# Expert lists two to eight: scattered to a table in memory instead of found by one-hot products

## The chip, the cores and the metric

One core of a Trainium2 chip runs the whole program. The metric is the device time in microseconds (us), median of several runs.

## The reference

Two stages on x of 4 x 512 rows of 512 numbers (2,048 tokens). The first adds a gated product of the normalised, FP8-rounded rows with an FP8-rounded context. The second, which the change concerns, is a mixture of experts: a router picks two of eight experts for every token, an expert takes at most 640 tokens in order of arrival, and each token gets back the gated sum of its experts' outputs.

```python
C = math.ceil(CAPACITY_FACTOR * S * K / E)           # 640
probs = jax.nn.softmax(xr @ Wg, axis=-1)
gate_vals, expert_idx = jax.lax.top_k(probs, K)
flat_e = expert_idx.reshape(-1)
oh = jax.nn.one_hot(flat_e, E, dtype=jnp.int32)
pos = jnp.sum((jnp.cumsum(oh, axis=0) - 1) * oh, axis=1)
kept = pos < C
...
dispatched = xr[dispatch_mask.reshape(-1) % S].reshape(E, C, d)
h = jax.nn.relu(jnp.einsum('ecd,edf->ecf', dispatched, w1))
expert_out = jnp.einsum('ecf,efd->ecd', h, w2)
```

So every expert needs a list: for each of its 640 slots, which token stands there and with what gate.

## The kernel before

The engines run in parallel, each through its own program, and meet at semaphores. TensorE is PE, VectorE is DVE, ScalarE is ACT, GpSimd is POOL, and SyncE is SP.

**The front** (to about 179 us) computes attention, norms and router. The lists come at its end. `choose` marks the two experts of each token; `place` counts on PE, which leaves each token's position in each expert; `places` and `gates` on DVE turn that into `slots` (position plus one, or 0) and `marks` (token number plus one, and the gate as a high and a low half float). The first expert's list is found apart: DVE writes 16 one-hot tiles (L1357), PE multiplies them with the marks (L589 the tokens, L599 the gates), `first_rows` and `first_gates` on DVE read the result.

**An expert** is one pass of a loop on all engines; the eighth pass is written out behind it. Its first part is 16 tiles of hidden units, f = 0 to 15. PE does 12 matmuls a tile (L817), ACT writes the high half of the result (L1102) and splits w2 (L1105), DVE writes the low half (L1534), the low half of w2 (L1537), and looks for the largest weight of the next expert's w1 (L1312). Within these tiles lies the search for the next expert's list: DVE compares slot numbers 1 to 640 with the tile's slots (`onehot_tile`, L1417), PE multiplies the one-hot with the marks of 128 tokens (`find`, 5 matmuls, L578).

The second part multiplies with w2 (`second`, L750), four slot groups of 128, with a small piece for the slots above 512 (`first_rows` L729, `turn_rows` L738, L790) if the expert has so many. `turn_rows` stands in the middle of the second group and waits for `low_rest` on DVE (L1552). DVE's order at the start of this part is: wait for the five `acc` gathers, copy the gates, `read_list` (L1424 to L1431), `w_scales` (L1299 to L1303, which waits for POOL's all-reduce of the weight peak), two reduces over w2 (`peak_w2`, L1316), `combine(0)` (L1547), `low_rest(0)`.

**POOL** works in the order that it is written in. Before the loop it gathers the first expert's rows (L448, five indirect DMAs of 128 rows) and the rows that its results are added to (L454, five more). A pass of the loop is: all-reduce of the w1 peak (L438), gather of the next expert's rows (L448), scatters of the results (L461), all-reduce of the w2 peak, and the gather of the rows for the next addition (L454). SP loads the weights of the next expert; its first load of that kind waits until the fifth row gather has landed.

At the end of the front DVE splits w1 of the first expert in four pieces (`low_w1`, L1321, 128 x 2048 each), two before `first_gates` and two behind it; PE needs all four, and four transposed slot groups (`turn_slots`, L609, copied by ACT), before the first tile.

Of the kernel before, what the change touches and what calls it, by code (L numbers as in the profile page):

```python
# [19 lines left out]
F32 = mybir.dt.float32  # L20
# [70 lines left out]
def build(nc, x, ctx_in, g_xattn, g_ffn, wg, w1, w2, out, xsplit):  # L91
    with ExitStack() as stack:
# [16 lines left out]
        w2_t = w2.rearrange("e (f p) d -> e p f d", p=P)  # L109
        wg_t = wg.rearrange("(k p) e -> p k e", p=P)  # L110
# [84 lines left out]
        slots = sb("slots", [P, E, NT], F32)  # L195
        marks = sb("marks", [P, E, NT, 3], F16)
        slot_now = sb("slot_now", [P, NT], F32)
        marks_now = sb("marks_now", [P, NT, 3], F16)
        onehot = sb("onehot", [P, 2, C], F16)
# [83 lines left out]
        pool_passed dve_passed pe_passed picked onehot_ready found_done found_read idx_ready  # L283
# [17 lines left out]
        FIND_STEPS, SCALE_STEPS = 3, 3  # L301
# [71 lines left out]
        def _(pool):  # L373
# [3 lines left out]
            for t, v in ((ident32, 0.0), (ident16, 0.0), (before, 0.0), (ones16, 1.0), (ones32, 1.0), (lower_e, 0.0),  # L377
                         (warm, 1.0)):
                last = nc.gpsimd.memset(t[:], v)
            last.then_inc(q["const_base"], 1)  # L380
            pool.wait_ge(q["const_base"], 1)
            for t in (ident32, ident16):
# [8 lines left out]
            nc.gpsimd.iota(marks[:, :, :, 0], [[0, E], [P, NT]], base=1, channel_multiplier=1,  # L391
# [74 lines left out]
            gather_x(0, first=True)  # L466
            pool.wait_ge(q["rows_out"], 16 * B)
# [22 lines left out]
        def _(pe):  # L490
# [82 lines left out]
            def find(n, i):  # L573
                if i == 0:
                    pe.wait_ge(q["found_read"], n + 1)
                pe.wait_ge(q["onehot_ready"], n * NT + i + 1)
                for s in range(NS):
                    mm = pe.matmul(found_ps[:, s, :], onehot[:, i % 2, s * P:(s + 1) * P], marks_now[:, i, :],  # L578
                                   start=(i == 0 and s == 0), stop=(i == NT - 1), skip_group_check=True)
                mm.then_inc(q["found_done"], 1)  # L580

            def find_rows(i0, i1):

                for i in range(i0, i1):
# [3 lines left out]
                    for s in range(NS):  # L588
                        mm = pe.matmul(found_ps[:, s, 0:1], first_onehot(i)[:, s * P:(s + 1) * P], marks[:, 0, i, 0:1],  # L589
                                       start=(i == 0 and s == 0), stop=(i == NT - 1), skip_group_check=True)  # L590
                    mm.then_inc(q["found_done"], 1)

            def find_gates():
# [3 lines left out]
                for i in range(NT):  # L597
                    for s in range(NS):
                        mm = pe.matmul(found_ps[:, s, 1:3], first_onehot(i)[:, s * P:(s + 1) * P], marks[:, 0, i, 1:3],  # L599
# [209 lines left out]
            def expert(e, last):  # L809
# [3 lines left out]
                for f in range(NF):  # L813
# [6 lines left out]
                    if not last:  # L820
                        find(e + 1, f)
# [312 lines left out]
        def _(dve):  # L1134
# [233 lines left out]
            def places():  # L1368
# [4 lines left out]
                V.scalar_tensor_tensor(slots[:, :, :].rearrange("p e i -> p i e"), place_ps[:, 0:NT, :], 1.0,  # L1373
                                       chosen[:, :, :], ALU.add, ALU.mult)
# [6 lines left out]
            def gates():  # L1381
# [7 lines left out]
                high = marks[:, :, :, 1].rearrange("p e i -> p i e")  # L1389
                prep.step(V.tensor_copy(high, prob[:, :, :]))  # L1390
                V.tensor_tensor(marks[:, :, :, 2].rearrange("p e i -> p i e"), prob[:, :, :], high,
                                ALU.subtract).then_inc(q["first_list"], 1)
# [13 lines left out]
            def pick(n, steps):  # L1406

                V.tensor_copy(slot_now[:, :], slots[:, bass.ds(n, 1), :].rearrange("p o i -> p (o i)"))
                V.tensor_copy(marks_now[:, :, :].rearrange("p i c -> p (i c)"),
# [220 lines left out]
```

## Time and profile before

| | us |
|---|---|
| median of 3 runs | 901.55 (901.01 to 903.36) |
| the profiled execution | 899.0 |
| its span, first to last instruction | 897.2 |
| PE busy | 822.8 (92%) |
| DVE busy | 643.1 (72%) |
| ACT busy | 365.4 (41%) |
| POOL busy | 196.5 (22%) |

The span lies 1.8 us under the time of the same execution. Busy times are those of instructions; an engine can have nothing to do and cost nothing, so the shares alone don't say what bounds the program.

### The profile page before, as it was taken

How to read it: one execution, taken by the hardware profiler on the slowest of the kernel's cores; microseconds unless marked ns; L12 is line 12 of the kernel's file. 1: busy time of each engine (PE TensorE's matmuls, PEld its weight loads, DVE VectorE, ACT ScalarE, POOL GpSimd, SP SyncE). 2: the span in 40 equal slices, each digit the busy share in tenths (PEclk: the TensorE clock that was granted, in tenths of full speed). 3: DMA queues.
4: the chain of work that ended last, by engine and by line, in shares of the span. 5: the costliest groups of instructions: out<-in, count | busy, mean ns of one | idle time of the engine just before them, and what ended most of it. 6: DMA issues, size and time to landing. Idle time of an engine off the chain costs nothing.

```text
span 897.2 us, 13430 instructions
## 1 busy us (share of the span) xinstructions
PE 822.8 (92%) x4809; PEld 400.3 (45%) x4810; DVE 643.1 (72%) x1119; ACT 365.4 (41%) x587; POOL 196.5 (22%) x165
## 2 busy tenths in 40 slices
PE   0287989499999999999999999999999999999996
PEld 0134558344444444444444444444444444444443
DVE  5999868768596877788688578857885878585530
ACT  3798996334133441444043414331432144224410
POOL 2132331500232023203220232023202320232001
PEclk9999996599999999999999999999999999999999
DMA  8600734382456266328542763265328532702000
GB/s 302 260 0 1 259 116 171 93 290 95 125 163 211 101 145 234 123 94 175 219 147 98 129 223 123 105 145 211 120 97 169 206 123 94 175 24 70 1 26 22
DMA packets 77753, 123.05 MB, mean 137 GB/s; under 512 B 41870, under 2 KB 41886, under 8 KB 73632
## 3 DMA queue, kind: packets, MB, share of 16 engines
q1 hardware_dynamic: 68032, 93.33, 32.4%
q0 software_dynamic: 9696, 29.39, 11.4%
q8 instruction: 15, 0.25, 0.1%
q14 instruction: 10, 0.08, 0.0%
HBM read 96.49 MB, written 18.87 MB: 129 GB/s over the span
## 4 chain that ended last, share of the span: by engine, by line
PE 80%; DVE 10%; ACT 4%; DMA 2%; issue 2%; POOL 1%; SPq 0%; DVEq 0%; POOLq 0%; ACTq 0%
PE mm L750 37%; PE mm L817 36%; PE mm L790 2%; PE mm L729 2%; PE marks_ps L578 1%; ACT region L874 1%; DVE region L1183 1%; DVE region L1194 1%; DVE region L1225 1%; DVE region L1221 1%; DMA gains<-in_g_ffn 1%; POOL region L448 1%; DMA w_stage<-in_L_ffn_w 1%; PE mm L521 1%; PE mm L549 1%
## 5 line engine op out<-in xcount | busy, mean ns | idle before, releaser
L817 PE MATMUL mm<-region,w_split 128*128 128x512 f16 x1536 | 347.7, 380 | 1.7 <-ACT region L971 1.4
L750 PE MATMUL mm<-region 128*128 128x512 f16 x1536 | 335.8, 379 | 0.0
L750 PEld LDWEIGHTS mm<-region 128*128 128x128 f16 x1536 | 148.2, 98 | 179.7 <-issue 4.5
L817 PEld LDWEIGHTS mm<-region,w_split 128*128 128x128 f16 x1536 | 142.3, 98 | 159.8 <-issue 3.8
L1102 ACT ACTIVATE region<-mm 128x512 f16<-128x512 f32 x128 | 76.4, 597 | 323.3 <-PE mm L817 323.3
L1534 DVE SCALAR_TENSOR_TENSOR region<-mm,region 128x512 f16<-128x512 f32 x128 | 88.5, 691 | 88.1 <-ACT region L1102 88.1
L461 POOL DMA_INDIRECT out<-region,back_now x40 | 64.9, 1623 | 168.6 <-DVE region L1547 141.3
L1537 DVE SCALAR_TENSOR_TENSOR region<-w_stage,w_scale,region 128x512 f16<-128x512 f32 x128 | 96.5, 754 | 0.0
L1105 ACT ACTIVATE region<-w_stage,w_scale 128x512 f16<-128x512 f32 x128 | 91.2, 712 | 0.0
L438 POOL PARTITION_ALL_REDUCE peak_all<-peak x14 | 4.9, 349 | 352.9 <-DVE peak L1292 299.1
L1312 DVE TENSOR_REDUCE top<-w_stage 128x1 f32<-128x512 f32 x112 | 75.9, 678 | 2.9 <-DMA w_stage<-in_L_ffn_w 2.9
L1321 DVE SCALAR_TENSOR_TENSOR w_split<-w_stage,w_scale,w_split 128x2048 f16<-128x2048 f32 x32 | 73.8, 2348 | 1.7 <-DVE region L1563 1.7
L1547 DVE SCALAR_TENSOR_TENSOR region<-mm,gate_now,region 128x512 f32<-128x512 f32 x32 | 23.9, 748 | 59.0 <-PE mm L750 58.9
L1316 DVE TENSOR_REDUCE top<-w_stage 128x1 f32<-128x2048 f32 x28 | 62.6, 2275 | 0.0
L859 ACT ACTIVATE w_split<-w_stage,w_scale 128x2048 f16<-128x2048 f32 x32 | 61.6, 1991 | 0.0
L1552 DVE SCALAR_TENSOR_TENSOR region<-mm,region 128x512 f16<-128x512 f32 x32 | 22.1, 691 | 54.1 <-ACT region L1113 54.1
L1113 ACT ACTIVATE region<-mm 128x512 f16<-128x512 f32 x32 | 19.2, 599 | 100.6 <-PE mm L729 60.4
L448 POOL DMA_INDIRECT region<-x_split,row_next x40 | 43.8, 1095 | 48.7 <-issue 25.2
L454 POOL DMA_INDIRECT region<-out,row_next x40 | 39.6, 990 | 29.1 <-DMA out<-region,back_now 19.0
L1417 DVE TENSOR_SCALAR onehot<-slot_iota,slot_now 128x640 f16<-128x640 f16 x112 | 42.1, 381 | 0.9
L578 PEld LDWEIGHTS marks_ps<-marks_now,onehot 128*128 128x128 f16 x560 | 30.4, 96 | 27.2 <-DVE onehot L1417 1.1
L874 ACT ACTIVATE region<-region 128x128 f32<-128x128 f32 x128 | 38.8, 388 | 4.2 <-DVE region L1188 4.1
(188 smaller groups left out, 620.9 us busy)
## 6 DMA issues: line engine op xcount, KB each, us to landing
w_stage<-in_L_ffn_w SPq DMA_DIRECT2D x64, 1024.0 KB, 5.4
region<-in_x SPq DMA_DIRECT2D x4, 1024.0 KB, 13.4
x_split<-region SPq DMA_DIRECT2D x8, 512.0 KB, 3.8
out<-region SPq DMA_DIRECT2D x4, 1024.0 KB, 7.4
w_stage<-in_ctx SPq DMA_DIRECT2D x2, 1024.0 KB, 12.4
region<-in_ctx SPq DMA_DIRECT2D x2, 1024.0 KB, 15.5
region<-x_split,row_next POOLq DMA_INDIRECT x40, 4.5
region<-out,row_next POOLq DMA_INDIRECT x40, 3.8
```

Of the source, the lines that this page charges most:

```text
L448: pool.indirect_dma_start(x_slots[:, s, :], None, xsplit, bass.IndirectOffsetOnAxis(ap=row_next[:, s:s + 1], axis=0)).then_inc(x_got[s], 16)
L461: pool.indirect_dma_start(out_rows, bass.IndirectOffsetOnAxis(ap=back_now[:, s:s + 1], axis=0), acc[:, s, :], None, bounds_check=S - 1, oo ...
L750: mm = pe.matmul(mm2[s % 2][:, :], hidden[:, hh, f, s * P:(s + 1) * P], w2_split[:, wh, f, :], start=(f == 0 and hh + wh == 0), stop=(f == ...
L817: mm = pe.matmul(products(f), w1_split[:, wh, k, f * P:(f + 1) * P], xT[:, xh * KD + k, 0:WIDE], start=(k == 0 and wh + xh == 0), stop=(k ...
L859: nc.scalar.activation(w1_split[:, 0, k, :], w1_stage[:, k, :], ACT.Copy, scale=w_scale[:, 0:1]).then_inc(q["w1_hi"], 1)
L1102: nc.scalar.activation(hidden[:, 0, f, 0:WIDE], products(f), ACT.Relu).then_inc(q["hidden_hi"], 1)
L1105: nc.scalar.activation(w2_split[:, 0, f, :], w2_stage[:, f, :], ACT.Copy, scale=w_scale[:, 1:2]).then_inc(q["w2_hi"], 1)
L1312: return V.tensor_reduce(top1[:, i:i + 1], part, X, ALU.max, apply_absolute_value=True)
L1316: return V.tensor_reduce(top2[:, k:k + 1], w2_stage[:, WF * k:WF * (k + 1), :].rearrange("p f d -> p (f d)"), X, ALU.max, apply_absolute_v ...
L1321: V.scalar_tensor_tensor(w1_split[:, 1, k, :], w1_stage[:, k, :], w_scale[:, 0:1], w1_split[:, 0, k, :], ALU.mult, ALU.subtract).then_inc( ...
L1534: V.scalar_tensor_tensor(hidden[:, 1, f, 0:WIDE], products(f), 0.0, hidden[:, 0, f, 0:WIDE], ALU.max, ALU.subtract).then_inc(q["hidden_don ...
L1537: V.scalar_tensor_tensor(w2_split[:, 1, f, :], w2_stage[:, f, :], w_scale[:, 1:2], w2_split[:, 0, f, :], ALU.mult, ALU.subtract).then_inc( ...
```

## The change

The one-hot search for experts two to eight is gone, on PE and on DVE. In its place every token writes two notes of 8 bytes (token number plus one, gate) into a table `lists` in memory, one entry for each expert and slot. Where a note goes is its code, expert times 640 plus position; `places` computes the codes, `notes_of_rows` on DVE picks the larger and the smaller one of each token with its gate, and POOL sends 32 indirect DMAs of 128 notes before the loop. The table is filled with zeros at the start. In the loop POOL loads one expert's 640 entries with a plain DMA at the top of a pass, and `read_list` reads them from there; it now stands behind `w_scales`. The first expert's list is found as before.

```diff
+            for i in range(NT):
+                for w in range(2):
+                    pool.indirect_dma_start(
+                        lists, bass.IndirectOffsetOnAxis(ap=goals[:, w, i:i + 1], axis=0), notes[:, w, i, :], None,
+                        bounds_check=E * C - 1, oob_is_err=False).then_inc(q["lists_out"], 16)
             pool.wait_ge(q["rows_out"], 16 * B)
-            pool.wait_ge(q["first_list"], 1)
             gather_acc()
+            pool.wait_ge(q["lists_out"], 16 * 2 * NT)
             with nc.gpsimd.Fori(0, E - 1) as e:
+                pool.dma_start(entries[:, :, :], lists_t[e + 1]).then_inc(q["entries_in"], 16)
                 weight_peak(0, e + 1)
...
-                    if not last:
-                        find(e + 1, f)
...
-                V.scalar_tensor_tensor(slots[:, :, :].rearrange("p e i -> p i e"), place_ps[:, 0:NT, :], 1.0,
-                                       chosen[:, :, :], ALU.add, ALU.mult)
+                prep.step(V.scalar_tensor_tensor(codes[:, :, :], place_ps[:, 0:NT, :], 1.0,
+                                                 first_code[:, :].unsqueeze(1).broadcast_to([P, NT, E]), ALU.add, ALU.add))
+                prep.step(V.tensor_tensor(codes[:, :, :], codes[:, :, :], chosen[:, :, :], ALU.mult))
...
+            def notes_of_rows():
+
+                prep.step(V.tensor_reduce(code_of[:, 0, :], codes[:, :, :], X, ALU.max))
+                prep.step(V.tensor_reduce(code_of[:, 1, :], codes[:, :, :], X, ALU.add))
+                prep.step(V.tensor_tensor(code_of[:, 1, :], code_of[:, 1, :], code_of[:, 0, :], ALU.subtract))
+                for w in range(2):
+                    here = here_gates[:, w, :, :]
+                    prep.step(V.tensor_tensor(here, codes[:, :, :], over(code_of[:, w, :], E), ALU.is_equal))
+                    prep.step(V.tensor_tensor(here, here, prob[:, :, :], ALU.mult))
+                    V.tensor_reduce(notes[:, w, :, 1], here, X, ALU.add)
+                prep.step(V.tensor_scalar(unused[:, :, :], code_of[:, :, :], 0.0, 2 * SKIP, ALU.is_equal, ALU.mult))
+                V.scalar_tensor_tensor(goals[:, :, :], code_of[:, :, :], -1.0, unused[:, :, :], ALU.add,
+                                       ALU.add).then_inc(q["notes_ready"], 1)
...
             first_gates()
+            notes_of_rows()
             low_w1(0, 2)
...
                 for f in range(NF):
-                    if not last and f + 1 < NT:
-                        onehot_tile(n, f + 1, n * NT + f)
...
                 if not last:
+                    w_scales(n, 0, e * 2 * SCALE_STEPS)
                     read_list(n)
-                    w_scales(n, 0, e * 2 * SCALE_STEPS)
```

On POOL, the end of the front and the top of the loop read as follows before. The bracket is what an instruction waits for; the first L438 row, marked ISA, stands ahead of the all-reduce itself and carries its wait.

```order
L448 DMA region<-x_split,row_next 128x1024 x4
L454 DMA region<-out,row_next 128x512 [waits first_list,rows_out]
L454 DMA region<-out,row_next 128x512 x4
L470 UNCONDITIONAL_BRANCH
L470 ISA
L438 ISA [waits peak1_in]
L438 ISA peak_all<-peak 128x1
```

And now:

```order
L461 DMA region<-x_split,row_next 128x1024 x4
L484 DMA lists<-notes,goals 5120x2 [waits notes_ready,zeros_in]
L484 DMA lists<-notes,goals 5120x2 x31
L467 DMA region<-out,row_next 128x512 [waits rows_out]
L467 DMA region<-out,row_next 128x512 x4
L490 UNCONDITIONAL_BRANCH [waits lists_out]
L490 ISA
L491 DMA entries<-lists 128x5x2
L451 ISA [waits peak1_in]
L451 ISA peak_all<-peak 128x1
```

The 32 notes stand between the two groups of gathers, and everything behind them on POOL, the all-reduce included, comes after them. On DVE, the start of an expert's second part before:

```order
L1580 TENSOR_TENSOR gate_rest<-gate_now,gate_rest 128x1 [waits now_ready]
L84 REGISTER_ALU
L1424 COPY found<-marks_ps 128x15 [waits found_done,now_ready]
L1425 REGISTER_ALU
L1426 TENSOR_SCALAR empty<-found 128x5 [waits found_read]
L1427 TENSOR_SCALAR row_next<-found 128x5
L1428 TENSOR_TENSOR gate_next<-found 128x5 [waits listed]
L1429 SCALAR_TENSOR_TENSOR back_next<-found,empty 128x5 [waits listed]
L1430 TENSOR_SCALAR gate_next<-gate_next,tanhs 128x5
```

And now, up to the reduce over w2:

```order
L1581 TENSOR_TENSOR gate_rest<-gate_now,gate_rest 128x1 [waits now_ready]
L84 REGISTER_ALU
L1309 TENSOR_SCALAR unit<-peak_all 128x1 [waits peak1_out,now_ready]
...
L1313 TENSOR_SCALAR w_scale<-w_scale 128x1 [waits scaling]
L1432 TENSOR_SCALAR empty<-entries 128x5 [waits entries_in]
L1433 TENSOR_SCALAR row_next<-entries 128x5
L1434 SCALAR_TENSOR_TENSOR back_next<-entries,empty 128x5 [waits listed]
L1435 TENSOR_SCALAR gate_next<-entries,tanhs 128x5
L84 REGISTER_ALU
L1436 TENSOR_SCALAR gate_next<-gate_next 128x5 [waits listed]
L1326 TENSOR_REDUCE top<-w_stage 128x1 [waits w2_in0]
```

The list is read behind the instruction that waits for the all-reduce, where it was read ahead of it.

## Rows read from the trace of the kernel before

**Rows 1.** The page: span, and the chain that ended last by engine.
```profile
span 897.2 us, 13430 instructions
...
PE 80%; DVE 10%; ACT 4%; DMA 2%; issue 2%; POOL 1%; SPq 0%; DVEq 0%; POOLq 0%; ACTq 0%
```
**Rows 2.** The chain in order of time (start, length, what), 255 to 280.
```profile
273.17 2.59 PE mm L817 x12
275.76 0.10 PE marks_ps L578 x5
```
**Rows 3.** The same chain over the whole span.
```profile
316.60 10.38 PE mm L750 x48
...
807.40 41.44 PE mm L817 x192
```
**Rows 4.** Groups by line: count, busy us, mean ns, idle before.
```profile
L461 POOL DMA_INDIRECT out<-region,back_now x40 | 64.9, 1623 | 168.6 <-DVE region L1547 141.3 <-DVE region L1563 21.7 <-issue 5.5
...
L1417 DVE TENSOR_SCALAR onehot<-slot_iota,slot_now 128x640 f16<-128x640 f16 x112 | 42.1, 381 | 0.9
L454 POOL DMA_INDIRECT region<-out,row_next x40 | 39.6, 990 | 29.1 <-DMA out<-region,back_now 19.0 <-issue 10.1
```
**Rows 5.** What L461 itself took, and its landing.
```profile
L461 POOL DMA_INDIRECT out<-region,back_now x40: 977/1034/2975, 242.8 to 892.1; - x40
...
DMA to landing us min/median/max: 2.1/4.2/10.0
```
**Rows 6.** POOL in order of time (start, length, line), end of the front.
```profile
169.05 2.90 POOL L448 DMA_INDIRECT region<-x_split,row_next  x1 [0.30 <-issue]
...
174.52 0.95 POOL L448 DMA_INDIRECT region<-x_split,row_next  x1 [0.30 <-issue]
```
**Rows 7.** DVE there, and its first wait in the first expert.
```profile
158.41 0.29 DVE L1378 TENSOR_REDUCE row_a<-region 128x16 f32<-128x128 f32 x1
...
168.51 0.24 DVE L1400 TENSOR_SCALAR gate_next<-gate_next 128x5 f32<-128x5 f32 x1
168.78 4.61 DVE L1321 SCALAR_TENSOR_TENSOR w_split<-w_stage,w_scale,w_split 128x2048 f16<-128x2048 f32 x2
...
188.47 0.69 DVE L1312 TENSOR_REDUCE top<-w_stage 128x1 f32<-128x512 f32 x1 [2.93 <-DMA w_stage<-in_L_ffn_w]
```
**Rows 8.** PE there.
```profile
176.73 1.03 PE L609 MATMUL mm<-ident,region 128*128 128x128 f16 x8 [1.30 <-DMA region<-x_split,row_next]
179.13 4.38 PE L817 MATMUL mm<-region,w_split 128*128 128x512 f16 x12 [1.36 <-ACT region L971]
...
190.10 2.76 PE L817 MATMUL mm<-region,w_split 128*128 128x512 f16 x12 [0.32 <-DVE region L1534]
```
**Rows 9.** DVE at the first expert's second part.
```profile
228.12 0.17 DVE L1292 TENSOR_REDUCE peak<-top 128x1 f32<-128x16 f32 x1
...
236.01 0.15 DVE L1299 TENSOR_SCALAR unit<-peak_all 128x1 f32<-128x1 f32 x1 [5.60 <-POOL peak_all L438]
...
241.76 0.68 DVE L1552 SCALAR_TENSOR_TENSOR region<-mm,region 128x512 f16<-128x512 f32 x1
```
**Rows 10.** POOL there.
```profile
235.60 0.38 POOL L438 PARTITION_ALL_REDUCE peak_all<-peak  x1 [53.87 <-issue]
```
**Rows 11.** PE there.
```profile
243.78 0.61 PE L738 MATMUL xT_ps<-ident,region 128*128 128x128 f16 x8
```
**Rows 12.** POOL's first plain DMA, 512 pieces of 32 bytes.
```profile
1.29 0.98 POOL L374 DMA_DIRECT2D wg_sb<-in_L_ffn_Wg  x1 [0.84 <-POOLq L1620]
```
**Rows 13.** PE's first matmul.
```profile
18.15 0.37 PE L497 MATMUL xT_ps<-region 128*16 128x128 f32 x1 [18.15 <-POOL marks L391]
```
**Rows 14.** DVE's first instruction that needs its result.
```profile
21.98 0.27 DVE L1200 TENSOR_REDUCE region<-xT_ps 16x1 f32<-16x128 f32 x1
```
**Rows 15.** The page: packets by size, and the DMA transposes' landing.
```profile
DMA packets 77753, 123.05 MB, mean 137 GB/s; under 512 B 41870, under 2 KB 41886, under 8 KB 73632
...
region<-region SPq DMA_TRANSPOSE x36, 6.2
```

More of the change, by code:

```diff
@@ L88, in end, with build @@
         assert self.n == self.steps, (self.n, self.steps)
-def build(nc, x, ctx_in, g_xattn, g_ffn, wg, w1, w2, out, xsplit):
+def build(nc, x, ctx_in, g_xattn, g_ffn, wg, w1, w2, out, xsplit, lists):
     with ExitStack() as stack:
@@ L194, in build @@
         row_a = sb("row_a", [P, NT], F32)
-        slots = sb("slots", [P, E, NT], F32)
-        marks = sb("marks", [P, E, NT, 3], F16)
+        codes = sb("codes", [P, NT, E], F32)
+        first_code = sb("first_code", [P, E], F32)
+        marks = sb("marks", [P, NT, 3], F16)
+        notes = sb("notes", [P, 2, NT, 2], F32)
+        goals = sb("goals", [P, 2, NT], I32)
+        code_of = sb("code_of", [P, 2, NT], F32)
+        unused = sb("unused", [P, 2, NT], F32)
+        zeros = sb("zeros", [P, 2 * E * C // P], F32)
+        here_gates = sb("here_gates", [P, 2, NT, E], F32)
+        entries = sb("entries", [P, NS, 2], F32)
         slot_now = sb("slot_now", [P, NT], F32)
-        marks_now = sb("marks_now", [P, NT, 3], F16)
-        onehot = sb("onehot", [P, 2, C], F16)
         found = sb("found", [P, NS, 3], F32)
@@ L390, in _ @@
                            allow_small_or_imprecise_dtypes=True)
-            nc.gpsimd.iota(marks[:, :, :, 0], [[0, E], [P, NT]], base=1, channel_multiplier=1,
+            nc.gpsimd.iota(first_code[:, :], [[C, E]], base=0, channel_multiplier=0,
+                           allow_small_or_imprecise_dtypes=True)
+            nc.gpsimd.iota(notes[:, :, :, 0], [[0, 2], [P, NT]], base=1, channel_multiplier=1,
+                           allow_small_or_imprecise_dtypes=True)
+            nc.gpsimd.iota(marks[:, :, 0], [[P, NT]], base=1, channel_multiplier=1,
                            allow_small_or_imprecise_dtypes=True).then_inc(q["consts"], 1)
@@ L571, in place @@
                 mm.then_inc(q["placed"], 1)
[L573 to L580, printed above, removed]
             def find_rows(i0, i1):
@@ L588, in find_rows @@
                     for s in range(NS):
-                        mm = pe.matmul(found_ps[:, s, 0:1], first_onehot(i)[:, s * P:(s + 1) * P], marks[:, 0, i, 0:1],
+                        mm = pe.matmul(found_ps[:, s, 0:1], first_onehot(i)[:, s * P:(s + 1) * P], marks[:, i, 0:1],
                                        start=(i == 0 and s == 0), stop=(i == NT - 1), skip_group_check=True)
@@ L598, in find_gates @@
                     for s in range(NS):
-                        mm = pe.matmul(found_ps[:, s, 1:3], first_onehot(i)[:, s * P:(s + 1) * P], marks[:, 0, i, 1:3],
+                        mm = pe.matmul(found_ps[:, s, 1:3], first_onehot(i)[:, s * P:(s + 1) * P], marks[:, i, 1:3],
                                        start=False, stop=(i == NT - 1), skip_group_check=True)
@@ L1526, in expert @@
                 n = e + 1
-                if not last:
-                    pick(n, e + 1)
-                    onehot_tile(n, 0, n * NT - 1)
                 for f in range(NF):
-                    if not last and f + 1 < NT:
-                        onehot_tile(n, f + 1, n * NT + f)
                     dve.wait_ge(q["hidden_hi"], e * NF + f + 1)
```

41 lines of the change are left out of this document (16 added, 25 removed).

## The prediction

> **What bounds the kernel now.** I read the page first. The chain of work that ended last runs through PE for 80% of the span, which is 897.2 us [rows 1]. The chain in order of time then shows how: within an expert PE goes from tile to tile, and the five matmuls of `find` lie on the chain between them, 0.10 us behind a tile of 2.59 [rows 2]. So PE's own queue is the bound from 179 us on, and what is taken from it is taken from the end, as long as nobody else becomes late. The front ends differently: PE waits there for the gathered rows and for DVE's split of w1 [rows 6 to 8]. That wait, and the first expert's second part, where POOL's first all-reduce is late already, are the two places to look at closely.
>
> **What goes from PE.** The last expert has no `find` and does its 16 tiles in 41.44 us; the second one starts at 273.17 and is done at 316.60, 43.43 us [rows 2, 3]. The difference, 1.99 us, is the price of 80 small matmuls in one expert. I take this instead of their busy time, since they overlap their neighbours. Seven experts make 13.9 us, of which six passes, 11.9 us, come after the first expert and meet no new work: POOL adds one plain DMA at the top of a pass, long before the list is read, and DVE loses 112 one-hots of 381 ns [rows 4], 2.7 us or more of 43, in a stretch where it has slack.
>
> In these six passes `read_list` (which the diff moves) stands behind `w_scales`. It is one copy and one addition shorter and the all-reduce it now stands behind has come by then, so `peak_w2` and `low_rest` start no later. The next rows are gathered some 0.4 us later, by an order that leaves them half an expert of time. Cost nothing; if that cover were gone it would be those 0.4 us seven times, 3 us.
>
> **What the front does.** At the start POOL gets a memset, a DMA and two more iotas, together under 2 us by the price of its first DMA [rows 12]. PE's first matmul waits for POOL at 18.15 [rows 13], but DVE looks at the result at 21.98 only [rows 14]: cost nothing, cover 3.4 us. `places` is one instruction longer, `gates` writes 16 elements where it wrote 128, which about cancel.
>
> `notes_of_rows` puts 11 instructions ahead of the second pair of L1321. A reduce over 128 elements takes 0.29 [rows 7], and 0.03 lies between one small instruction and the next (168.51 + 0.24 to 168.78 [rows 7]). Eight at 0.3 and three small ones at 0.2 make 3.0 us. This pair ended at 168.78 + 4.61 = 173.4; now it ends at 176.2, which is still ahead of the first tile at 179.13 [rows 8]. PE did not wait for DVE there but for the fourth group of rows, at 176.73 [rows 8].
>
> Those rows will come earlier, and that is the less obvious half. A row gather started at 169.05, just behind the start of an L1321, and took 2.90; one started at 174.52, with no L1321 running, took 0.95 [rows 6, 7]. The first of the pair ends about 171.1, half way through 4.61, so the gather was held until then and needed 0.8 more. With 3 us of short instructions in place of L1321, gathers three and four run at about 1.25 us each: the fourth ends near 171.4 instead of 174.2 (the fifth's start less 0.30), and its group is transposed before 175. Then w1, at 176.2, is the last thing PE waits for, and the first tile starts about 176.6 instead of 179.1: a gain of 2.5 us. The fifth gather comes 0.7 to 2.8 us earlier too, and with it SP's load of the next w1, for which DVE waited until 188.47 and PE's fourth tile until 190.10. Tiles two and three end 1.2 us before that (183.5 + 2 x 2.7 = 188.9). I count 0.7 of these as gained.
>
> The Trainium skill (SBUF — State Buffer, Who interferes with whom) has a rule on this: a DVE instruction with two inputs in SBUF contends with GpSimd instructions that read SBUF, but descriptor generation needs only the write side, which such an instruction leaves free. L1321 has two such inputs, and the gather beside it took three times its own time. By the rule, notes would never be held and cost 0.05 us less each, 1.6 us for all; by the rows, a few are held.
>
> **What POOL gets.** A gather without trouble is 0.95 with 0.30 in front of it [rows 6]. A scatter with a bounds check, as the notes have, is 1.03 in the median [rows 5]. Beside an expert's tiles, where DVE's two-input instruction L1537 is short, L454 averages 0.99 against 0.95 [rows 4]: 0.05 for collisions. So a note is 1.03 + 0.05 + 0.30 = 1.38 us. The bounds: 1.25 (the plain gather), and 1.62 + 0.30 = 1.92, by the mean of the scatters [rows 4], most of whose excess is from L1321. I take 1.38, since the notes run beside tiles.
>
> The sum on POOL's queue: the fifth gather ends about 174.8; the first note is held by the last L1321 until 177.1; 31 more at 1.38 end at 219.9; five gathers for the addition at 1.30 end at 226.4. The wait for all notes is over by then (they land some 4.2 behind their issue [rows 5]). The entries' DMA has 640 pieces; one of 512 took 0.98 [rows 12], so POOL stands at the all-reduce at 227.7. Before, the peak was there at 228.3 and the all-reduce ended at 235.98, though POOL had been idle for 53.87 us [rows 9, 10]: 7.7 us after its wait was over, of which 0.38 is the operation. The ISA instruction ahead of it carries the wait, so this first-time cost cannot be paid early, and I expect it again in full: the all-reduce ends near 235.3.
>
> DVE in turn: before, `w_scales` began at 236.01 and `low_rest(0)` ended at 241.76 + 0.68 = 242.44; PE needed that at 243.78 [rows 9, 11]. Slack, 1.3 us. `read_list` used to lie in the wait and now lies behind it, 0.8 us. So `low_rest(0)` ends at 242.44 - 0.7 + 0.8 = 242.5, and PE turns its rows at 242.6. Without POOL it would do so at 243.78 - 2.5 - 0.7 - 2.0 = 238.6. Of 5.2 us gained so far, PE gives 4.0 back waiting for DVE, and 1.2 are left. Behind this place DVE's work goes by PE's again.
>
> **The sum.** 1.2 + 11.9 = 13.1 us. The span becomes 884.1 and its execution 885.9 (1.8 more, as before). The profiled execution was 2.5 under the median, so I take the same 13.1 off the median: 901.55 - 13.1 = 888.4.
>
> **The rivals.**
>
> *The notes just fit.* At 1.25 a note and no collisions they end at 215.9, the gathers at 222.4, the entries (0.6) at 223.4, and the peak is there at 223.1. PE doesn't wait: 16.8 us, 884.7. For it: the spacing of consecutive gathers. Against: the bounds check's 0.08 shows in every quiet scatter.
>
> *Notes of 1.45 to 1.7 us.* Each 0.1 us more is 3.2 us later on POOL and, the slack being used up, on PE: 890.5 to 898.6. For it speaks that L1321's sisters hold POOL for their whole length; against, that five gathers beside tiles averaged under 1.0.
>
> *Slower: the notes are the bound.* The place is POOL's queue between the two groups of gathers. What has to be lost is 13.1 us over 32 notes, 0.41 each: from 1.79 us a note on the change costs time, at 1.92 it is 905.7. It could also come from the DMA engines: 4,096 packets of 8 bytes, eight to an engine in each note. The nearest row is the transposes': 41,870 packets under 512 bytes, nearly all of the 36 transposes, 73 to an engine, landed in 6.2 us, so at most 0.085 us a packet [rows 15], 0.7 us a note and hidden. At 0.22 us a packet they would be the bound.
>
> The skill speaks against this change here (DMA: Bandwidth & Descriptors, Specifications and Rules for kernel authors): under 512 bytes a transfer is a read-modify-write, and many small ones should be one large one. By its fit of about 2.0 us of fixed cost per DMA (Anatomy of one DMA), with none overlapping, 32 notes would be an estimated 64 us and the change would lose some 7 us; its share is within the 0.10 for slower below. Scatters landed in 4.2 us in the median while gathers followed each other every 1.25 [rows 5, 6], so I take what a DMA costs after its issue as overlapped.
>
> *No change.* `find` would have to lie in time that PE doesn't have otherwise. The last expert speaks against that directly.
>
> **Chances and range.** The forecast 0.60 (885.5 to 892), the fitting notes 0.12, the dearer notes 0.15, slower 0.10, no change 0.03. A measurement of this kernel tells about 0.3% from none, 2.7 us. Faster 0.86, same 0.04 (the last and the edge of the dearer notes), slower 0.10. The range leaves out the slower case and the dearest notes above, and about nothing below: 884 to 896.
>
> **What would show it.** Right: no L578 and tiles 2.59 us apart; L817's first start near 176.6; 32 POOL rows of 1.0 to 1.1 from 175 to 220; the all-reduce at about 235, still some 7 us behind POOL's arrival; PE idle some 4 us before its turning matmuls in the first expert and nowhere in the other six. Wrong: notes of 1.5 and more; an all-reduce without its 7 us (then PE waits for nobody, 885); a first tile still at 179, which costs nothing more, since POOL's queue sets that part; or tiles that stay 2.7 apart, the largest term.

## The result, and the profile after

| | before | after |
|---|---|---|
| median, us | 901.28 (900.21 to 903.36, 4 runs) | 886.93 (886.21 to 887.49, 4 runs) |
| the profiled execution | 899.0 | 887.49 |
| its span | 897.2 | 885.8 |
| PE busy | 822.8 | 809.4 |
| POOL busy | 196.5 | 236.1 |

The ratio is 0.9838, with an interval of 0.9821 to 0.9854: 14.35 us less, where 13.1 were forecast (888.4). The first chip of the runs below gives the same. On the second the change made the kernel 2.1% **slower**, and that became the main question.

The chain that ended last in the profile after, in order of time (start, length, what), here the first and the last whole run of tiles:

```profile
271.59 41.44 PE mm L829 x192
...
793.74 41.44 PE mm L829 x192
```

The pieces of `find` between the tiles are gone, and 16 tiles take 41.44 us in experts two to eight (43.87 in the first, whose early tiles wait). From the second expert's first tile to the last one's it was 534.23 us [rows 2, 3]; now it is 793.74 - 271.59 = 522.15. That is 12.08 us, where 11.9 were forecast.

POOL in order of time after the notes, with what ended the idle time ahead of each instruction in the bracket; the notes themselves (L484) are the 32 rows before:

```profile
218.31 0.99 POOL L467 DMA_INDIRECT region<-out,row_next  x1 [0.30 <-issue]
...
225.11 0.94 POOL L491 DMA_DIRECT2D entries<-lists  x1 [0.70 <-issue]
234.25 0.38 POOL L451 PARTITION_ALL_REDUCE peak_all<-peak  x1 [8.20 <-issue]
```

The same instructions of the notes as a group (shortest, median and longest in ns), and how long POOL stood ahead of them:

```profile
L484 POOL DMA_INDIRECT lists<-notes,goals x32: 982/982/2131, 174.6 to 217.0; - x32
...
  issue: 9.7, 32
```

A note takes 0.98 to 1.00 us and 0.30 ahead of it; from the third (179.23) to the last (217.01) they follow each other every 1.30 us. Only the first two were held for long (the last L1331 ends at 178.05). The all-reduce came 8.20 us behind the entries' DMA and did not wait for its data: DVE's peak stood ready at 225.55 + 0.17.

PE in the first expert:

```profile
178.86 44.03 PE L829 MATMUL mm<-region,w_split 128*128 128x512 f16 x192 [2.16 <-DVE loads L1427]
222.73 10.52 PE L762 MATMUL mm<-region 128*128 128x512 f16 x48
...
242.19 0.62 PE L750 MATMUL xT_ps<-ident,region 128*128 128x128 f16 x8 [0.94 <-DVE region L1553]
```

The first tile now waits for DVE's chain (w1's last split, then `loads`), no longer for the rows, and `turn_rows` waits 0.94 us for `low_rest`, which stands behind the all-reduce.

### The profile page after: what moved, and what is told of

Same layout as the page of the kernel before. It is cut to its first block, busy times and chain, and to the rows that moved or that the text cites. A ratio compares the mean times of both kernels' runs of the same rounds, so it can differ in the third digit from the quotient of the medians.

```text
span 885.8 us, 12028 instructions
## 1 busy us (share of the span) xinstructions
PE 809.4 (91%) x4249; PEld 386.9 (44%) x4250; DVE 607.6 (69%) x991; ACT 365.4 (41%) x587; POOL 236.1 (27%) x208
## 4 chain that ended last, share of the span: by engine, by line
PE 76%; DVE 10%; POOL 5%; issue 4%; ACT 3%; DMA 1%; POOLq 0%; DVEq 0%; ACTq 0%
PE mm L762 36%; PE mm L829 33%; POOL lists L484 3%; PE mm L542 2%; PE mm L802 2%; ACT region L884 1%; PE mm L741 1%; DMA gains<-in_g_ffn 1%; DVE region L1193 1%; DVE region L1204 1%; DVE region L1235 1%; DVE region L1231 1%; PE mm L570 1%; POOL region L461 1%; PE xT_ps L570 1%
## 5 line engine op out<-in xcount | busy, mean ns | idle before, releaser
L829 PE MATMUL mm<-region,w_split 128*128 128x512 f16 x1536 | 335.3, 381 | 2.2 <-DVE loads L1427 2.2
L829 PEld LDWEIGHTS mm<-region,w_split 128*128 128x128 f16 x1536 | 150.8, 98 | 185.3 <-issue 5.7
L474 POOL DMA_INDIRECT out<-region,back_now x40 | 64.0, 1599 | 169.4 <-DVE region L1548 140.2
L1331 DVE SCALAR_TENSOR_TENSOR w_split<-w_stage,w_scale,w_split 128x2048 f16<-128x2048 f32 x32 | 73.8, 2347 | 1.7 <-DVE region L1564 1.7
L461 POOL DMA_INDIRECT region<-x_split,row_next x40 | 41.2, 1029 | 53.4 <-issue 27.8
L467 POOL DMA_INDIRECT region<-out,row_next x40 | 41.6, 1039 | 28.8 <-DMA out<-region,back_now 18.7
L484 POOL DMA_INDIRECT lists<-notes,goals x32 | 34.0, 1063 | 9.7 <-issue 9.7
## 6 DMA issues: line engine op xcount, KB each, us to landing
w_stage<-in_ctx SPq DMA_DIRECT2D x2, 1024.0 KB, 13.9
```

Of the source, the lines that this page charges most:

```text
L474: pool.indirect_dma_start(out_rows, bass.IndirectOffsetOnAxis(ap=back_now[:, s:s + 1], axis=0), acc[:, s, :], None, bounds_check=S - 1, oo ...
L484: pool.indirect_dma_start(lists, bass.IndirectOffsetOnAxis(ap=goals[:, w, i:i + 1], axis=0), notes[:, w, i, :], None, bounds_check=E * C - ...
L829: mm = pe.matmul(products(f), w1_split[:, wh, k, f * P:(f + 1) * P], xT[:, xh * KD + k, 0:WIDE], start=(k == 0 and wh + xh == 0), stop=(k ...
L1331: V.scalar_tensor_tensor(w1_split[:, 1, k, :], w1_stage[:, k, :], w_scale[:, 0:1], w1_split[:, 0, k, :], ALU.mult, ALU.subtract).then_inc( ...
```

## The experiments

They ran in four groups, each with the kernel before on the same chip. By its time there the chips are told apart: **chip one** (before 900.59 us), **chip two** (909.58 and 908.35), **chip three** (900.66).

**The kernels as they stand, once more.** The change on chip one:

> The changed kernel again, unaltered, as the measure for the runs beside it, and a second profile of it. Its first profile had everything from the first tanh on some 1.8 us later than the profile of before (the landing of the second gate's load took 9.50 us where it had taken 7.90) and a tail behind the last matmul of 9.0 us where it had been 6.8. If both are scatter between executions, this profile shows other values; if the change makes them (its zero fill follows those loads on POOL's queue), both stand again. Time: 887 us, within 1.

886.61 us, ratio to the kernel before 0.9838, with an interval in brackets [0.982, 0.9857]. This is the base for chip one. Its profile has the first tile at 177.86, POOL's all-reduce at 233.39 and PE waiting 0.80 us at `turn_rows`.

**e1: `find`'s matmuls put back on PE, and nothing else.**

```diff
                     mm.then_inc(q["mm1_done"], 1)
+                    if not last:
+                        for s in range(NS):
+                            pe.matmul(found_ps[:, s, :], ident16[:, :], ones16[:, 0:3], ...)
```

> The changed kernel with five small matmuls (128 x 128 weights, 3 columns) put back behind each of the 16 tiles of experts one to seven, on constant operands, with nothing waiting for them. Theory: PE's queue is the bound and these cost what the search cost, 2.0 us an expert: 14 us slower than the changed kernel less the 0.9 us that PE waits in the first expert, so +13. Rival: the search cost PE little by itself and what was gained came from the waits for one-hots and from DVE's freed time: then +0 to +4 us.

899.68 us, ratio 0.9989 [0.9979, 1.0]: 13.1 us over the change. PE in order of time:

```profile
193.87 0.27 PE L834 MATMUL marks_ps<-ones,ident 128*128 128x3 f16 x5
194.00 2.75 PE L829 MATMUL mm<-region,w_split 128*128 128x512 f16 x12
196.58 0.27 PE L834 MATMUL marks_ps<-ones,ident 128*128 128x3 f16 x5
```

Tiles start 2.71 us apart again. On this chip the gain is the place of these 560 small matmuls on PE; all the rest of the change, gains and losses together, comes to 0.9 us (900.59 - 899.68).

**e2: one all-reduce more, early, on POOL,** in a stretch where it has nothing to do (behind `low_rows(2)`, ahead of the first row gather).

```diff
             low_rows(2)
+            nc.gpsimd.partition_all_reduce(warm_all[:, :], first_code[:, 0:1], P, bass.bass_isa.ReduceOp.max)
```

> The changed kernel with one more all-reduce on POOL, on a constant, in the idle time ahead of the first row gathers. Theory: the 7.5 us or so between POOL's arrival at the first all-reduce and its start are a first-use cost that hangs on the operation and can be paid early: the first expert's all-reduce comes at about 227 and not 234, and PE's 0.94 us of waiting before its turning matmuls goes: -0.9 us against the changed kernel. Rival: the delay belongs to the place (the loop's start, or the DMAs ahead), it stands again and the time is the same. Second rival: the early all-reduce pushes the code of the gathers out, which are then late by some 7 us, and the time grows by that.

885.15 us, ratio 0.9821 [0.9807, 0.9835], 1.5 us under the change; the two intervals overlap, so the time alone doesn't settle it. POOL does:

```profile
147.86 0.38 POOL L448 PARTITION_ALL_REDUCE warm_all<-first_code  x1 [6.11 <-issue]
...
224.01 0.95 POOL L493 DMA_DIRECT2D entries<-lists  x1 [0.70 <-issue]
225.00 0.31 POOL L453 PARTITION_ALL_REDUCE peak_all<-peak  x1
232.52 1.03 POOL L463 DMA_INDIRECT region<-x_split,row_next  x1 [7.20 <-issue]
```

The 6 to 9 us are paid once, wherever the first all-reduce stands. With that done early, the one that DVE waits for came right behind the entries instead of 8.73 us later, and PE's idle time at `turn_rows` is gone. (The 7.20 ahead of the gather is the wait for DVE's `read_list`, done at 231.44; all but 1.1 of it is that, so nothing is paid again.) The Trainium skill (GPSIMD Engine Reference, Instruction dispatch) gives about 6 us for the first call to freshly loaded code on GpSimd, with no instruction in the profile to show it. The trace agrees for the early one, 6.11 us; where the all-reduce stands behind DMAs it took 8.20 and 8.73 (6.42 in e9), and no run here shows what the rest is.

**e3: `notes_of_rows` behind the last two pieces of w1** instead of ahead of them.

```diff
             first_gates()
-            notes_of_rows()
             low_w1(0, 2)
             low_w1(0, 3)
             list_loads()
+            notes_of_rows()
```

> The changed kernel with the 11 instructions that make the notes moved behind the second pair of w1 splits and the loads. Theory: each row gather that starts beside such a split is held to its end and 0.8 us more; gathers three and four are held again as in the kernel before, the fourth group reaches PE at about 178.3 instead of 175.7, and the first tile starts at 180.7 instead of 178.9: +1.8 us, although DVE is done with w1 3 us earlier. Rival: DVE's chain alone sets the start: the first tile comes 2 to 3 us earlier; since the all-reduce on POOL follows later, -0 to -1 us in time.

889.17 us, ratio 0.9873 [0.9853, 0.9893], 2.6 over the change. POOL:

```profile
169.73 2.91 POOL L461 DMA_INDIRECT region<-x_split,row_next  x1 [0.30 <-issue]
172.94 1.96 POOL L461 DMA_INDIRECT region<-x_split,row_next  x1 [0.30 <-issue]
175.20 0.95 POOL L461 DMA_INDIRECT region<-x_split,row_next  x1 [0.30 <-issue]
178.00 1.02 POOL L484 DMA_INDIRECT lists<-notes,goals  x1 [1.86 <-DVE goals L1414]
```

The gathers take what they took before [rows 6], since L1331 again runs beside them (169.46 to 174.07); the first tile starts at 179.64. So the order of DVE's code, not the work, gave the front its 1.8 us (the change has its first tile at 177.86 there). The time itself is 2.6 over because the notes start later, at 178.00, and with them the all-reduce: 235.93, where the change has 233.39 there. In the change the same three gathers took 0.95 each beside the short instructions of `notes_of_rows`. The Trainium skill (SBUF — State Buffer, Who interferes with whom) leaves descriptor writing free beside an instruction of this kind, but has it hold a GpSimd instruction that reads SBUF. A gather by index takes its row numbers (`row_next`) from SBUF, so the 2.91 against 0.95 fits the second half and not the first; which of the two holds for a plain DMA no run here shows.

**The kernels on chip two.** e4 to e7 below ran there, and both kernels too:

> The kernel before once more, for a second profile: where its first tanh stands (10.75 us in the first), how long the tail behind the last matmul is (6.8 us), and that the first expert's all-reduce again starts some 7 us behind its peak.

> The changed kernel once more. Three kernels that hold its 32 notes (with more notes, with the zero fill elsewhere, with one-hots back) were run on another chip of the same kind and came out 2 to 3% slower than the kernel before there, with PE standing 11 us at a time while the notes were sent, waiting for nothing that the profile shows. Theory: that is the notes' doing, and depends on the chip: on a chip where the kernel before takes about 909 us this one takes 920 to 930, with such waits between the first note and a few us behind the last; on one where it takes about 901 it takes 887. Rival: it was the three edits: 887 to 895 on any chip.

Before: 908.34 (span 906.5). The change: 927.19 us, ratio 1.0206 [1.0176, 1.0236]. POOL sends its notes at the same rate as on chip one, and is done at the same time (the last at 216.13). PE, though, in order of time:

```profile
177.24 9.35 PE L829 MATMUL mm<-region,w_split 128*128 128x512 f16 x36 [2.17 <-DVE loads L1427]
187.23 5.35 PE L829 MATMUL mm<-region,w_split 128*128 128x512 f16 x24 [0.64 <-issue]
194.59 2.76 PE L829 MATMUL mm<-region,w_split 128*128 128x512 f16 x12 [2.01 <-issue]
202.36 5.25 PE L829 MATMUL mm<-region,w_split 128*128 128x512 f16 x12 [5.01 <-issue]
214.36 4.38 PE L829 MATMUL mm<-region,w_split 128*128 128x512 f16 x12 [6.74 <-issue]
228.44 22.30 PE L829 MATMUL mm<-region,w_split 128*128 128x512 f16 x96 [9.70 <-DVE region L1535]
250.58 10.52 PE L762 MATMUL mm<-region 128*128 128x512 f16 x48
```

For the first ten or so notes all is well. Then PE does one tile in 8 to 14 us instead of 2.59, with idle times that end on "issue", and goes on at 228.44, 4 us after POOL's stream of notes and gathers is over (224.4). The stretches of 10 us show who works (engine, busy us, instructions; then granted clock, DMA share, GB/s):

```profile
196.00:206.00 10.00, 4.99 (x16) 1.74 (x14) 1.96 (x3) 1.21 (x2) 7.56 (x9) 0.73 0.51 106
206.00:216.00 10.00, 3.26 (x8) 0.89 (x7) 1.96 (x3) 1.21 (x2) 7.70 (x8) 0.67 0.02 1
```

The columns are PE, weight loads, DVE, ACT, POOL. Eight matmuls in 10 us, and the DMA engines nearly idle: 1 GB/s. So it is neither bandwidth nor POOL's queue. Part of the loss is the clock: with a granted share of 0.73 and 0.67, partly at the lower level (1.2 GHz), behind PE's idle times, the tile from 202.36 takes 5.25 us where others take 2.76. On chip one the same stretch reads:

```profile
206.00:216.00 10.00, 10.00 (x48) 4.52 (x47) 7.47 (x13) 4.82 (x8) 7.86 (x8) 1.00 0.43 104
```

Which engine waits for which is seen when their rows stand side by side. ACT reads a tile's products when PE is done with it, DVE follows ACT, and PE may start a tile when DVE is done with the one two before. ACT and DVE on chip two:

```profile
200.99 0.60 ACT L1112 ACTIVATE region<-mm 128x512 f16<-128x512 f32 x1 [6.57 <-remote]
212.98 0.60 ACT L1112 ACTIVATE region<-mm 128x512 f16<-128x512 f32 x1 [10.79 <-remote]
213.61 0.69 DVE L1535 SCALAR_TENSOR_TENSOR region<-mm,region 128x512 f16<-128x512 f32 x1 [10.04 <-ACT region L1112]
227.07 0.60 ACT L1112 ACTIVATE region<-mm 128x512 f16<-128x512 f32 x1 [12.88 <-remote]
```

"Remote" is a wait that ends with a semaphore's increment for which the profile finds no sender. ACT's three rows belong to the tiles f = 4, 5 and 6, which PE had done at 192.58, 197.36 and 207.62: ACT starts 8.4, 15.6 and 19.5 us later, and each time 0.03 us behind the increment, which the trace has at 200.96, 212.96 and 227.04. In the same kernel on chip one ACT starts 0.04 us behind PE in all 16 tiles. The other steps are as quick as ever: DVE starts 0.03 us behind ACT (213.58, 213.61), PE 0.06 behind DVE (214.30, 214.36). So the "issue" waits of L829 are waits for DVE, and the whole stall is one step, PE's increment reaching ACT. (The ends of matmuls are modelled, but PE had started f = 5 at 194.59, before the increment of f = 4 came.) Instructions that come late are not the reason for these waits: ACT, DVE and PE each go on at once when their increment is there.

A second trace of the same thing: a note's DMA makes 16 increments of `lists_out`, 512 in all. The traces on chips one and three record 511 or 512 of them, those on chip two 93 to 124. POOL's wait for all of them was over in time (its entries' DMA started at 223.45), so they counted; why so few are recorded there is open.

The kernel before has losses of its own on chip two. PE's waits of both kernels there, first before, then the change (line, total us, times, longest):

```profile
PE mm L729 <- issue: 4.6, 10, 1.0
```

```profile
PE mm L829 <- issue: 14.4, 4, 6.7
...
PE mm L829 <- DVE region L1535: 9.7, 1, 9.7
PE mm L741 <- issue: 4.7, 8, 1.0
```

L729 and L741 are the first matmuls of the small piece (the slots above 512). In the passes that have it they run while POOL sends five gathers and a scatter back to back. In the kernel before:

```profile
592.33 0.94 POOL L448 DMA_INDIRECT region<-x_split,row_next  x1 [0.30 <-issue]
593.58 1.03 POOL L461 DMA_INDIRECT out<-region,back_now  x1 [0.30 <-issue]
```

```profile
591.70 2.55 PE L729 MATMUL mm<-w_split,region 128*32 128x512 f16 x42
594.47 0.42 PE L729 MATMUL mm<-w_split,region 128*32 128x512 f16 x3 [0.22 <-issue]
595.19 0.38 PE L729 MATMUL mm<-w_split,region 128*32 128x512 f16 x1 [0.30 <-issue]
```

The holes open about 7 us into that burst and close behind it. A pass with them takes 92.9 us (537.78 to 630.65) against 91.04 on the other chip (534.13 to 625.17), and four such passes are most of why the kernel before is 8 us longer here. It isn't shown that this is a small form of the stall: no hand-over is due between these matmuls, and two passes without the small piece take 85.0 us each on both chips, although POOL sends the same burst. The late increment itself shows in that kernel too, beside the first expert's gathers: ACT's L1113 starts 2.04 us behind PE's L729 (242.19 behind 240.15), on the other chip 0.14.

**e4: eight notes more,** to tables that nobody reads, one behind every fourth.

```diff
+                if i % 2 == 0:
+                    pool.indirect_dma_start(
+                        spare[i // 2], bass.IndirectOffsetOnAxis(ap=goals[:, 0, i:i + 1], axis=0), notes[:, 0, i, :],
+                        None, bounds_check=E * C - 1, oob_is_err=False).then_inc(q["lists_out"], 16)
```

> The changed kernel with eight notes more (the first note of every second group of 128 tokens is also written to tables that nobody reads), 40 indirect DMAs in place of 32. Theory: POOL's queue sets the first all-reduce and PE waits for it already, so each further note costs PE its full 1.29 us: +10.3 us, all in PE's wait before the turning matmuls of the first expert. Rival: there is slack behind POOL and the wait of 0.94 us is something else: less than +5 us. Second rival: the small writes back up in the DMA engines: over 1.29 us a note and more than +10.3.

939.68 us, ratio 1.034 [1.0321, 1.0359], on chip two: 12.5 over the change there, 1.6 us a note. PE stood still longer by what the stream was longer:

```profile
223.58 5.30 PE L833 MATMUL mm<-region,w_split 128*128 128x512 f16 x12 [17.52 <-issue]
240.41 24.82 PE L833 MATMUL mm<-region,w_split 128*128 128x512 f16 x108 [11.53 <-DVE region L1539]
```

It resumes at 240.41 instead of 228.44, and again by way of ACT: ACT starts on f = 4 28.3 us behind PE. The expectation reckoned with POOL's queue alone; the size came out near it for another reason.

**e5, e6, e7: three other suspects, on chip two.** e5 fills the table later (`zeros` sent behind `context_up(3)`), e6 puts the one-hots back on DVE as work that nobody reads, e7 makes an entry of the table 512 bytes instead of 8 (and sends the longer fill where e5 does):

```diff
-        lists, ..., notes[:, w, i, :], None,
+        lists, ..., notes_wide[:, 2 * (w * NT + i):2 * (w * NT + i) + P], None,
```

> The changed kernel with the zero fill of the table issued by POOL in the middle of the front and not at the start. Theory: its 41 KB at the start are nothing beside the inputs; the first profile's 1.8 us of later start are scatter: same time within 0.5 us. Rival: the fill and its memset delay the gates' landing: 1.5 to 2 us faster, and the first tanh at about 10.8 us in the profile.

> The changed kernel with one one-hot comparison (128 x 640) a tile put back on DVE in experts one to seven, unread. Theory: DVE had slack within the tiles and its freed 42 us were worth nothing; the comparison also holds POOL's notes at times: +0 to +1 us. Rival: DVE's relief is a good part of the gain: +3 us and more.

> The changed kernel with entries of 512 bytes in the table in place of 8: a note carries its 8 bytes and 504 bytes that nobody reads, the zero fill (2.6 MB) is sent in the middle of the front. Theory: the DMA engines are held by writes under 512 bytes, and code for the other engines waits behind them: with 512 bytes the waits without a cause go, and the time is that of the kernel before less 13 us whatever the chip, perhaps 1 us more for the bytes. Rival: it is the count of pieces, 4,096 of them, or the table's scattered rows, not their size: same time as the changed kernel on the same chip, or more.

926.96 us (ratio 1.021 [1.0184, 1.0236]), 928.08 (1.0204 [1.018, 1.0228]) and 928.4 (1.0216 [1.0182, 1.0251]), against 927.19 for the change. All the same, all with the same stall. The fill's place is worth nothing that these times could show; the one-hots were free on DVE, as forecast, though that is measured on this chip alone; and the size of a piece does nothing: with 512 bytes PE stalls 6.61 and 14.83 us ahead of two tiles, as with 8. The Trainium skill (DMA: Bandwidth & Descriptors, Specifications) has transfers under 512 bytes as read-modify-writes; what holds PE up here is not that.

**e8: no notes at all,** so that experts two to eight have empty lists (their products run on row 0, their scatters write nothing).

> The change without its 32 notes: experts two to eight get empty lists (their products run all the same on row 0, their scatters write nothing), so that part of the computation is left out, and nothing else of the order changes. Theory (the notes' stream on POOL holds up the instructions of PE, ACT and DVE, and that alone turns the gain into a loss on the chip where the kernel before takes 908 to 909 us): there the tiles of the first expert come every 2.59 us again and the idle times that end on 'issue' before them (14.4 us on PE mm L829 in the change there) are gone; the first part shrinks by about 27 us and the time is about 898, ratio 0.985 to 0.992. On the chip where the kernel before takes 900 to 901 us the notes cost only POOL's time ahead of the all-reduce, whose wait for PE was 0.8 us, so 885 to 887. Rival (the loss on that chip comes from the table's other steps, the load of the entries and the lists of the experts, or from the order of the code): 920 to 928 there.

It ran on chip three: 884.51 us, ratio 0.9816 [0.9798, 0.9833]. So on a chip like the first the notes cost some 2 us in all (886.61 on chip one; the intervals of the two ratios overlap). Its PE goes from the first tile to `turn_rows` in 239.61 - 177.75 = 61.86 us without a wait; in the change it is 63.33. What it would do on chip two was not measured, though that was the question.

**e9: the notes in four bursts of eight.**

```diff
             for i in range(NT):
+                if i % 4 == 0 and i:
+                    pool.wait_ge(q["hidden_done"], i // 4 * 5)
```

> The same 32 notes in four bursts of 8 (10.3 us each); the second, third and fourth wait for the halves of tiles 5, 10 and 15 of the first expert. Theory A (a long unbroken stream is what holds the other engines up: in the change on the chip of 908 us the first ten notes went by before PE's first 'issue' wait): with gaps of some 3 to 7 us the tiles come nearly every 2.59 us again; POOL's last note ends near 229 instead of 217, all-reduce near 245 instead of 234, PE waits some 5 to 8 us more before the turning of rows than the change does on the good chip: time about 900 to 908 where the kernel before takes 908, and 891 to 896 where it takes 901. Theory B (each note takes from the others' supply whether or not there are gaps): the stall stays at about 27 us, time 925 to 935 on the chip of 908. On the chip of 901 both say 891 to 896, since there the notes held nobody up.

896.34 us, ratio 0.9938 [0.9917, 0.996], on chip three as well. The part on chip two stays open; what it shows is POOL's path on a good chip. The all-reduce moved to 241.72, and PE:

```profile
249.66 1.03 PE L752 MATMUL xT_ps<-ident,region 128*128 128x128 f16 x8 [8.91 <-DVE region L1555]
...
250.62 7.47 PE L764 MATMUL mm<-region 128*128 128x512 f16 x24
```

POOL is 8.3 us later at the all-reduce than on chip one (233.39), and so is PE at `turn_rows` (249.66 against 241.33). The 24 matmuls behind it take 7.47 us instead of 5.34, at a mean granted clock of 0.63 between 249 and 257, where the change has 1.00 (the full 2.4 GHz) in 241 to 249. So a stretch at the lower level follows the 9 us in which PE did nothing, and that is 2 us more.

## Why the prediction was right, and where it would not have been

**PE's 13.9 us of `find`: right.** 12.08 in six passes (11.9 forecast), and e1 gives back 13.1 in all.

**The front: right in mechanism, smaller in size.** DVE's short instructions freed the gathers: 0.95 each, as forecast, and e3 takes it away again. `notes_of_rows` took 2.9 us (3.0). The first tile came at 178.86, not 176.6. About 2 us of that lie ahead of it all: PE's first matmul waits 20.0 us where it waited 18.15 [rows 13], and in the execution on chip one the tile starts at 177.86. The rest is `loads`, which stands behind w1's split on DVE and which PE waits for; the sum had left it out. The prediction said that a late first tile costs nothing more, since POOL sets that part, and so it was, with 0.94 us of PE's wait left over.

**A note: mis-sized.** 1.30 us, not 1.38. Of the bounds check's 0.08 at most 0.05 showed (0.98 to 1.00 against a gather's 0.95), and of collisions only the two held ones and one of 1.27. The notes ended at 218.01 instead of 219.9. The 4,096 packets weren't there either: eight notes more (e4) add 256 packets to the page's count, 32 a note or 1,024 for all, so a piece is not a packet of its own in it.

**The first all-reduce: right that it is paid behind the notes, wrong that it cannot be paid early.** It took 8.2 + 0.38 us instead of 7.7, which ate half of what the notes had gained (POOL was there at 226.05, not 227.7); it was over at 234.63 (235.3 forecast). The step read the wait on the instruction ahead of the all-reduce as the reason why the cost comes late; e2 shows an earlier all-reduce paying it.

**PE's wait: 0.94 us, not 4.0.** The end of it was right: PE turns its rows at 242.19 (242.6). It waited less because it had come later, 2.3 us with the first tile and 0.4 from there to `turn_rows`. From here on the gain was 1.6 us against 243.78 [rows 11], where 1.2 was forecast.

**A loss that the sum did not have.** 1.59 + 12.08 makes 13.67 at the last expert's first tile (807.40 to 793.74), but the spans differ by 11.4. Behind the last scatter (L474, over at 879.41) the program takes 6.4 us to its end, where it took 4.1 behind 893.07. On chip two it is 6.4 and 4.1 as well, so it belongs to the change. 2.0 of the 2.3 us are one instruction, the DRAIN with which POOL ends its program (before, then the change):

```profile
L92 POOLq DRAIN  x1: 1786/1786/1786, 895.2 to 895.2; - x1
```

```profile
L92 POOLq DRAIN  x1: 3741/3741/3741, 881.8 to 881.8; - x1
```

It took 1.79 us in both profiles of the kernel before and 3.74 in all three of the change, on either chip. The notes don't do it, since without them (e8) it took 4.15; what of the change does is open.

**How near 13.1 was.** The spans differ by 11.4 us and the medians by 14.35: the profiled execution of before lay 2.3 under its median, that of the change 0.6 over. A front 2.3 us later than forecast was covered by PE's wait, and the tail's 2.3 had no term. So the terms for PE are confirmed one by one, and that the total came so near is in part luck. In the rival of the fitting notes 5.2 and 11.9 make 17.1, where the text has 16.8. And on chip two the forecast would have failed by 39 us.

**The slower rival.** Its place was right, its mechanism was not. It asked what the notes cost POOL's queue (from 1.79 us a note on) or the DMA engines in bytes and packets. On chip two the notes followed each other at the same rate and the DMA engines were nearly idle. What grew was the time from PE to ACT, between 187 and 228. From first tile to L802 the change took 97.6 us there (177.24 to 274.80), the kernel before 71.6 (179.67 to 251.23, its L790): 26.0 lost, 2.4 won ahead of it, 6.8 won in the passes, 2.4 lost at the end. That makes the 19.1 between the spans, but for rounding. The passes win 6.8 and not 12.1 because the four with the small piece lose 13.0 us on chip one's in the change, and 7.8 in the kernel before. The prediction could not have read any of it: its trace has no such wait.

**What is shown of the cause, and what is not.** The stall begins some 10 us into POOL's unbroken stream of indirect DMAs and ends about 3 us behind it (ACT's last long wait ends at 227.07); it grows with their number (e4), not with their bytes (e7), nor with the fill or DVE's load (e5, e6). It sits in one step, PE's increments reaching ACT. The Trainium skill (Runtime: NRT & Kernel Launch, Instruction fetch mechanics) says that an engine's instructions come by a DMA queue of their own; that these fetches stand behind POOL's pieces is what the expectation of e7 supposes. The trace speaks against it for the stall, since all three engines go on at once when the increment comes; for the holes within L729 and L741 it can't be excluded. What delays the increments is open. A rival that no run separates is the notes' own increments, 16 a DMA: e4 has more of them, e7 as many. Open too are why the other chips have none of it, and whether gaps between the notes would help.

## What to carry to other kernels

Small work that stands in the queue of the engine that is always busy is worth its whole time; take it off, even if another engine gets three times as much. But ask of a long train of indirect DMAs not only what it costs its own queue: measure on more than one chip, and look for waits on "issue" or "remote" on engines that have nothing to do with it. Then lay the engines' rows side by side, one hand-over after the other: here it was one of three that was late. A first all-reduce costs 6 to 9 us once; put one where GpSimd idles (885.15 here, the shortest complete version on chip one).

## What the runs showed of the hardware

- On one of three chips (on the third, the notes ran in bursts only), PE's increments reach ACT up to 19.5 us late (33 with eight notes more) while 32 indirect DMAs of 128 pieces go out back to back, against 0.04 us on the others: tiles 8 to 14 us apart instead of 2.59, with DMA at 1 GB/s. DVE behind ACT and PE behind DVE are as quick as ever (0.03 and 0.06 us).
- The same chip runs the kernel before 8 to 9 us longer, with holes of up to 1.0 us in PE's L729 in the four later passes that have it.
- It records 93 to 124 of the 512 increments that the notes make, the other chips 511 or 512.
- The stall is the same with pieces of 8 and of 512 bytes (927.19 and 928.4 us).
- The first all-reduce costs 6.1 to 8.7 us wherever it stands, and later ones follow in their turn.
- POOL's closing DRAIN took 1.79 us in the kernel before and 3.74 in the change (4.15 without the notes).
